# Second mixture of experts in tiles that serve two experts: 144 tiles in place of 160

## What is computed

```python
x = x + L0_gnn(layernorm(x), adj)
x = x + L0_ffn(layernorm(x))      # 8 experts, the two best of each row
x = x + L1_gnn(layernorm(x), adj)
x = x + L1_ffn(layernorm(x))      # 32 experts, the best of each row

def L1_ffn(x):
    idx = argmax(x @ router_w.T + router_b, axis=-1)
    h = relu(einsum('nd,ndh->nh', x, W1[idx]) + b1[idx])      # 128 -> 32
    return relu(einsum('nh,nhd->nd', h, W2[idx]) + b2[idx])   # 32 -> 128
```

## Time and profile before

| | us |
|---|---|
| median of 3 executions (1197.79 to 1203.39) | 1198.93 |
| the profiled execution, its time | 1197.08 |
| its span, first to last instruction | 1195.3 |
| TensorE busy in the span | 948.1 (79%) |
| VectorE busy | 791.0 (66%) |
| ScalarE busy | 708.2 (59%) |
| GpSimd busy | 781.6 (65%) |
| mean granted clock of TensorE, share of full speed | 0.837 |

### The profile page before, as it was taken

The page is one execution under the profiler, slowest core; times in us unless marked ns, Lnnn a source line. Parts: engine busy times, 40 slices in busy tenths (PEclk is TensorE's granted clock), DMA queues, the critical chain, the costliest instruction groups (busy, mean ns, idle before and its releaser), DMA issues. The chain is left out here.

```text
span 1195.3 us, 27365 instructions
## 1 busy us (share of the span) xinstructions
PE 948.1 (79%) x6789; PEld 839.2 (70%) x6789; DVE 791.0 (66%) x3492; ACT 708.2 (59%) x2414; POOL 781.6 (65%) x989
## 2 busy tenths in 40 slices
PE   5888988887179999999994899999960667666873
PEld 4677877776079999999994688888850555544653
DVE  6688898889459999999994378888873121121221
ACT  3998898886035656555552899999930333322431
POOL 4357777777617787877776048778785366666666
PEclk9999897987579999999997999999975655666555
DMA  9133432211367777777772113232213442223210
GB/s 207 37 120 118 139 102 61 60 51 38 95 180 207 203 205 206 208 203 207 196 203 60 36 51 87 76 86 76 60 42 109 109 111 83 74 82 85 64 35 8
DMA packets 147913, 130.88 MB, mean 109 GB/s; under 512 B 26450, under 2 KB 119484, under 8 KB 147760
## 3 DMA queue, kind: packets, MB, share of 16 engines
q1 hardware_dynamic: 125456, 93.02, 30.4%
q0 software_dynamic: 18272, 34.21, 8.4%
q10 hardware_dynamic: 4032, 1.89, 0.5%
HBM read 83.28 MB, written 49.61 MB: 111 GB/s over the span
## 5 line engine op out<-in xcount | busy, mean ns | idle before, releaser
L477 POOL DMA_INDIRECT xs<-staged,dst x256 | 258.9, 1011 | 77.6 <-issue 68.5
L1067 ACT ACTIVATE hT<-bank,wt 128x128 f32<-128x128 f32 x620 | 177.2, 369 | 133.4 <-PE bank L1274 81.4
L528 POOL DMA_INDIRECT out<-oq,xq x160 | 159.9, 999 | 112.2 <-DVE oq L978 66.3
L506 POOL DMA_INDIRECT x2d<-ob,xi x155 | 163.6, 1055 | 43.3 <-issue 29.1
L1260 PE MATMUL bank<-xnT,wt 128*128 128x128 f32 x1240 | 166.9, 278 | 0.7 <-issue 0.4
L1274 PE MATMUL bank<-w2s,hT 128*128 x1240 | 165.5, 276 | 0.7 <-DVE ob L951 0.5
L978 DVE SCALAR_TENSOR_TENSOR oq<-bank,xq 128x512 f32<-128x512 f32 x40 | 27.7, 692 | 197.1 <-remote 103.2
L1260 PEld LDWEIGHTS bank<-xnT,wt 128*128 128x128 f32 x1240 | 152.6, 194 | 3.1 <-issue 2.5
L1274 PEld LDWEIGHTS bank<-w2s,hT 128*128 128x128 f32 x1240 | 150.9, 192 | 1.8 <-issue 1.2
L1101 ACT ACTIVATE xnqT<-bank 128x512 f32<-128x512 f32 x40 | 23.9, 596 | 164.0 <-remote 71.0
L1016 ACT ACTIVATE p<-bank,nm 128x128 f32<-128x128 f32 x256 | 103.1, 403 | 19.1 <-DVE nm L699 13.9
(11 more groups left out here) (202 smaller groups left out, 2313.9 us busy)
## 6 DMA issues: line engine op xcount, KB each, us to landing
wt<-wpd SPq DMA_DIRECT2D x155, 258.0 KB
xq<-xs SPq DMA_DIRECT2D x160, 66.0 KB
xi<-xs SPq DMA_DIRECT2D x155, 66.0 KB
xb<-x2d SPq DMA_DIRECT2D x32, 258.0 KB
xb<-in_x SPq DMA_DIRECT2D x32, 256.0 KB
wpd<-w1c SPq DMA_DIRECT2D x56, 129.0 KB
xs<-staged,dst POOLq DMA_INDIRECT x256
out<-oq,xq POOLq DMA_INDIRECT x160
```

The costliest lines, as they stand in the source:

```text
L477: pool.indirect_dma_start(out=xs[l], out_offset=bass.IndirectOffsetOnAxis(ap=dst[b % ND][:, c:c + 1], axis=0), in_=stag[s][:, q, 0:ROW], i ...
L506: pool.indirect_dma_start(out=x2d, out_offset=bass.IndirectOffsetOnAxis(ap=xi[t % NXI][:, ID:ID + 1].bitcast(U32), axis=0), in_=ob[:, t % ...
L528: pool.indirect_dma_start(out=orow, out_offset=bass.IndirectOffsetOnAxis(ap=xq[j % NXQ][:, q, ID:ID + 1].bitcast(U32), axis=0), in_=oq[j % ...
L1067: last = act.activation(hT[t % 2][:, j, :], HID[t % 2][:, j, :], ACT.Gelu, bias=wt[t % NW][:, c:c + 1])
```

## The change

Two experts form a unit: the bucket of the even one grows down and that of the odd one grows up from the same point, so that they meet without a gap, and only the unit as a whole has a partly filled tile. 16 units give (16384 - 16) / 128 + 16 = 143 tiles, rounded up to 144, or 36 quads; there are 16 fills. A tile may hold rows of both experts. So each tile is worked out for both: the first matmuls have 97 output rows (32 of the one expert, 1 for the bias row, then 64 onward for the other), the second matmuls are done for rows 0 to 32 and for rows 64 to 96 of `hqT` into banks of their own, and VectorE multiplies each by the row's flag (`WLO` is 1 - odd, `WHI` is odd) and adds them. The flags are computed in `route1` and put into `staged` in `places`. The weights are packed by unit, W1, b1 and W2, b2 side by side, and ScalarE copies all 226 columns of a unit into `vq`, from which TensorE takes both operands' weights.

```diff
-NTILE = (NTOK // P + NB[0] - 1, NTOK // P + NB[1])
+NU = (NB[0], E1 // 2)
+NTILE = ((NTOK - NU[0]) // P + NU[0], ((NTOK - NU[1]) // P + NU[1] + 3) // 4 * 4)
+NFILL = (NB[0], E1 // 2)
+SPFILL = (16, 9)
-VW = H1 + 1 + P
+HW = 64 + H1 + 1
+VW = HW + 1 + P
-        vt = sb("vt", [P, E1, VW])
+        vt = sb("vt", [P, E1 // 2, VW])
-        NXQ, NOQ, NVQ = 12, 8, 5
+        NXQ, NOQ, NVQ = 10, 5, 4
-        TQ, HQ, YQ = bank[0], bank[1:3], bank[3:5]
+        TQ, HQ, YQ = bank[0], bank[1:3], (bank[3:5], bank[5:7])
...
-                for s in range(2):
-                    dve.memset(hqT[s][H1:H1 + 1, :], 1.0)
+                dve.wait_ge(sem("vt_zero"), 1)
+                dve.memset(vt[H1:H1 + 1, :, HW], 1.0)
+                dve.memset(vt[64 + H1:HW, :, HW], 1.0).then_inc(sem("vt_one"), 1)
...
                 dve.tensor_tensor(ge3(oh, k, E), rows(rev, k, E), wide(k1, k, E), ALU.is_equal).then_inc(sem("oh"), 1)
+                link(dve.tensor_copy(oddi[:, 0:k * G], k1[:, 0:k * G]))
+                link(dve.tensor_scalar(oddi[:, 0:k * G], oddi[:, 0:k * G], 1, None, ALU.bitwise_and))
+                mark(dve.tensor_copy(odd[:, 0:k * G], oddi[:, 0:k * G]))
...
+                    settled()
...
+                        dve.tensor_scalar(staged[:, s:s + run, :, WLO], t, -1.0, 1.0, ALU.mult, ALU.add)
+                        dve.tensor_copy(staged[:, s:s + run, :, WHI], t)
...
                     after(dve, "yq", j)
+                    for q in range(G):
+                        dve.tensor_scalar(ta_q[:, q, :], ya_q[:, q, :], row[:, q, WLO:WLO + 1], None, ALU.mult).then_inc(sem("ta_q"), 1)
+                    for q in range(G):
+                        after(dve, "ta_q", G * j + q)
+                        op = dve.scalar_tensor_tensor(tb_q[:, q, :], yb_q[:, q, :], row[:, q, WHI:WHI + 1], ta_q[:, q, :],
+                                                      ALU.mult, ALU.add)
+                    op.then_inc(sem("tb_q"), 1)
...
-                    dve.scalar_tensor_tensor(oq[j % NOQ][:, :, :], YQ[j % 2][:, :].rearrange("p (g f) -> p g f", g=G), 0.0, xq[j % NXQ][:, :, 0:P], ALU.max,
+                    after(dve, "tb_q", j)
+                    dve.scalar_tensor_tensor(oq[j % NOQ][:, :, :], tb_q[:, :, :], 0.0, row[:, :, 0:P], ALU.max,
                                              ALU.add).then_inc(sem("oq"), 1)
...
-                after(act, "hq_ps", j - NVQ)
-                after(act, "hqT", j - NVQ)
+                after(act, "yq", j - NVQ)
-                    last = act.activation(vq[j % NVQ][:, q, :], vflat[:, bass.ds(expert[4 * (j % 2) + q], H1 + 1)], ACT.Copy)
+                    last = act.activation(vq[j % NVQ][:, q, :], vflat[:, bass.ds(expert[4 * (j % 2) + q], VW)], ACT.Copy)
...
-                    if j % 2 == 0:
-                        expert = column(mybir.EngineType.PE, 1, 1, 4 * j, (E1 - 1) * VW)
-                    for q in range(4):
-                        last = pe.matmul(YQ[j % 2][:, q * P:(q + 1) * P], hqT[j % 2][0:H1 + 1, q * P:(q + 1) * P],
-                                         vflat[0:H1 + 1, bass.ds(expert[4 * (j % 2) + q] + (H1 + 1), P)], start=(q == 0), stop=(q == 3),
-                                         skip_group_check=True)
+                    for h in range(2):
+                        rows_ = slice(64 * h, 64 * h + H1 + 1)
+                        for q in range(4):
+                            last = pe.matmul(YQ[h][j % 2][:, q * P:(q + 1) * P], hqT[j % 2][rows_, q * P:(q + 1) * P],
+                                             vq[j % NVQ][rows_, q, HW + 1:VW], start=(q == 0), stop=(q == 3),
+                                             skip_group_check=True)
...
-                        last = pe.matmul(HQ[j % 2][0:H1, q * P:(q + 1) * P], vq[j % NVQ][:, q, 0:H1],
+                        last = pe.matmul(HQ[j % 2][0:HW, q * P:(q + 1) * P], vq[j % NVQ][:, q, 0:HW],
```

More of the change, by code:

```diff
@@ L226, in program @@
         filli = [sb(f"filli{l}", [P, E1], I32) for l in range(2)]
+        cntu = sb("cntu", [P, NU[1]])
         tabf = [sb(f"tabf{l}", [P, 4, 2]) for l in range(2)]
         tab = [sb(f"tab{l}", [8, P], I32) for l in range(2)]
-        hqT = [sb(f"hqT{s}", [H1 + 1, T]) for s in range(2)]
+        hqT = [sb(f"hqT{s}", [HW, T]) for s in range(2)]
         with ExitStack() as early:
@@ L272, in program @@
         xnqT = sb("xnqT", [P, T])
[L274 removed]
+        vq = [sb(f"vq{s}", [P, G, VW]) for s in range(NVQ)]
+        ta_q = sb("ta_q", [P, G, P])
+        tb_q = sb("tb_q", [P, G, P])
         oq = [sb(f"oq{s}", [P, G, P]) for s in range(NOQ)]
[L276 removed]
+        TQ, HQ, YQ = bank[0], bank[1:3], (bank[3:5], bank[5:7])
         def numbers(engine, ap, top):
@@ L311, in load, with fills @@
                 sp.dma_start(xb[n % NX][:, :, 0:(P, XW)[l]], xg[l][g]).then_inc(sem(f"x_in{n % NX}"), 16)
-            def fills(l, half):
+            def fills(l):
                 sp.wait_ge(sem("fill_row"), l + 1)
-                for r in numbers(mybir.EngineType.SP, filli[l][0:1, 16 * half:min(16 * half + 16, NB[l])], DUMMY[l] - P):
+                for r in numbers(mybir.EngineType.SP, filli[l][0:1, 0:SPFILL[l]], DUMMY[l] - P):
                     sp.dma_start(xs[l][bass.ds(r, P), :], pad[:, :]).then_inc(sem(f"filled{l}"), 16)
@@ L363, in _ @@
                                      w1c[:, pairs[k][h], :]).then_inc(sem("wpd"), 16)
-            fills(0, 0)
+            fills(0)
             scattered(0)
@@ L384, in _ @@
                 load(n)
-            fills(1, 0)
+            fills(1)
             scattered(1)
@@ L640, in numbers_ready @@
                 link(dve.tensor_copy(regf[:, :], regi[:, :]))
-                for l in range(2):
-                    dve.tensor_copy(first[l][:, :, 0], regf[:, 0:NB[l] // 2])
-                    dve.tensor_scalar(first[l][:, :, 1], regf[:, 0:NB[l] // 2], -1.0, -(REGION - 1.0), ALU.mult, ALU.add)
+                dve.tensor_copy(first[0][:, :, 0], regf[:, 0:NB[0] // 2])
+                dve.tensor_scalar(first[0][:, :, 1], regf[:, 0:NB[0] // 2], -1.0, -(REGION - 1.0), ALU.mult, ALU.add)
+                dve.tensor_scalar(first[1][:, :, 0], regf[:, :], -1.0, -(NTOK - 1.0), ALU.mult, ALU.add)
+                dve.tensor_scalar(first[1][:, :, 1], regf[:, :], float(NTOK), None, ALU.add)
                 dve.memset(sgn[:, :, 0], 1.0)
@@ L794, in tile_table @@
                 sh = shift[:, :, :].rearrange("p a b -> p (a b)")[:, 0:B]
[L795 to L798, removed]
+                U = NU[l]
+                if l == 0:
+                    link(dve.tensor_tensor(fillf[:, 0:B], end, s, ALU.mult))
+                    dve.tensor_tensor(filli[l][:, 0:B], fillf[:, 0:B], sh, ALU.add).then_inc(sem("fill_row"), 1)
+                    link(dve.tensor_tensor(cnt[:, 0:B], end, f, ALU.subtract))
+                    link(dve.tensor_scalar(cnti[:, 0:B], cnt[:, 0:B], P - 1.0, None, ALU.add))
+                else:
+                    ends = end.rearrange("p (k b) -> p k b", b=2)
+                    dve.tensor_copy(filli[l][:, 0:U], ends[:, :, 1]).then_inc(sem("fill_row"), 1)
+                    link(dve.tensor_tensor(cnt[:, 0:B], end, f, ALU.subtract))
+                    counts = cnt[:, 0:B].rearrange("p (k b) -> p k b", b=2)
+                    link(dve.tensor_tensor(cntu[:, 0:U], counts[:, :, 0], counts[:, :, 1], ALU.add))
+                    link(dve.tensor_scalar(cnti[:, 0:U], cntu[:, 0:U], P - 1.0, None, ALU.add))
+                B = U
                 for c in range(2):
```

64 lines of the change are left out of this document (43 added, 21 removed).

## The result

The changed kernel takes 1229.4 us (median of 4 runs, 1224.97 to 1230.72) beside 1199.35 us of the kernel before: 1.023 times as long, 95% interval 1.021 to 1.025. It is slower, as forecast, but by 30 us where 72 had been forecast. The profiled execution took 1228.77 us, its span is 1227.0.

The account below looks back on a forecast made before the run. The last stage was taken to be bound by a TensorE-VectorE loop in which no step overlaps another, 6.22 us per quad, not by GpSimd. 983 + 32 times the new 9.0 us loop gave 1271 us, range 1200 to 1325.

Parts of the forecast that it names:

- 9.0 us per quad: Last stage: the new loop of 8.44 us at the lower clock, + 1.0 for late completions, - 0.4 for the clock.
- 0.25 each, + 2.00 in the loop: Last stage, TensorE: eight further second-matmul passes per quad at 0.25 us each add 2.00 us to the loop.
- the halves overlap in the array: Rival: second matmuls stay near 2.1 us, loop 6.4 + 0.8 us, 1213 us in all; chance 0.06.
- late completions "+ 1.0": Last stage: matmul consumers starting late cost 1.32 us per quad before; less a quarter, 1.0 us is carried over.
- "- 0.4" for the clock: Last stage: with 16% of the time at the higher clock level, a quad gets 0.4 us shorter.
- The chain: Last stage, VectorE: four multiplications and four multiply-adds out of PSUM before `oq` add 1.94 us to the loop.
- Graph layer + 8.5: Second graph layer: added small routing operations cost 0.53 us, times 16, + 8.5 us; bounds 3 and 13.
- The head's - 1.3: Start of the kernel: the memset of `vt` has fewer columns, 4.38 to 3.07 us, saving 1.3 us.
- Seam - 5.5: Between graph layer and last stage: 16 fills for 32 end near 914, first load 5.5 us earlier; bounds - 4 and - 8.
- First rounds + 4: Start of the last stage: first `oq` comes 12.0 us after the first `xnq`, 8.0 before, so + 4.
- Copies, buffers and wider first matmuls at 0: Last stage: ScalarE's wider copies, fewer buffers and 97-column first matmuls lie off the loop and cost 0.
- TensorE stays at the higher clock: Rival, last stage: the loop is 5.77 us and the time 1168 us, faster than before; chance 0.10.

Follow-up runs that it names:

- e11: Changed kernel with the second matmuls ordered tile, then row half, so the halves alternate; 1202.6 us, 1.002 of a before of 1200.6.
- e8: Changed kernel without the second matmuls of rows 64 to 96, the second expert's product left out; 1180.9 us, 1.038 of a before of 1138.7.
- e10: Changed kernel with `xnq` ahead of the chain, second matmuls' row halves alternating and four flag operations for five; 1192.1 us, 0.993 of a before of 1200.6.
- e7: Kernel before plus eight VectorE operations of 128 columns per quad between second matmuls and `oq`; 1180.7 us, 1.036 of a before of 1138.7.
- the first set: The first runs of both kernels, with stalls: changed kernel 1229.4 us beside 1199.35 us of the kernel before.
- e6: The changed kernel, unchanged, run again in a set without stalls; 1214.3 us, 1.066 of a before of 1138.7.
- e5: The kernel before, unchanged, run again for its profile in a set without stalls; 1138.5 us.
- e9: Changed kernel with three more 16-bit matmuls of 512 columns per quad in TensorE's idle time; 1205.3 us, 1.006 of a before of 1200.6.
- e2: Changed kernel with TensorE's register loads back and the second matmuls of rows 0 to 32 reading W2 at a register's address; 1211.8 us, 1.065 of before.
- e3: Changed kernel with the next quad's `xnq` issued on VectorE ahead of the flags' chain; 1132.9 us, 0.997 of a before of 1137.1.
- e16: The edit of e7 repeated, one execution, on the chip number of e9 to e11; 1180.2 us beside a before of 1138.6.
- e17: Kernel before with `xnq` issued ahead of `oq`, one execution on the chip number of e9 to e11; 1137.9 us beside a before of 1138.6.

## Why the prediction was half right

*Direction and mechanism: right.* The loop, its order and what waits for what are as forecast; four rounds fewer don't pay for longer ones. TensorE stays at the lower clock (0.51) with idle time in each round. What was off is the size: three terms of the 9.0 us per quad were mis-sized, and the change cost 30 us for 72.

*The step that failed most: the second matmuls at "0.25 each, + 2.00 in the loop".* They took 3.13 us to the chain and not 4.12, so 0.99 us per quad, 32 us over 32 rounds. The prediction had a single boundary between the row halves pay off, where the trace has eight of the sixteen passes side by side (four of either half, started in pairs). The rival "the halves overlap in the array", at 0.06, was half true as the code stands and wholly true in e11. The Trainium skill (TensorE: Matmul & The Clock Gate, Part 3) says that weight loads overlap running matmuls of other rows; e8 and e11 agree (the eight further passes cost 1.03 us as the code stands and nothing when the halves alternate), and the reading that this touches only one boundary was the prediction's own.

*The second failed step: late completions "+ 1.0" carried over, and "- 0.4" for the clock.* Neither came, a net 0.6 us per quad or 19 us. An amount that couldn't be explained was treated as a property of the code, and the runs show it to be one of some sets, which strikes the kernel before and e10 but not the changed kernel's steady loop. This is also why the difference is 30 us there and 75.6 us elsewhere. That the forecast of + 72 comes near the second number is luck: its loop was 1.2 us too long, and its base was a before of 1197. The - 0.4 was carried over from the granted clock of 0.58 in the kernel before; in the changed kernel the clock is 0.51, so hardly a round has the higher level.

*The chain was sized too short*: 2.27 us for 1.94, + 0.33 per quad, 11 us. A multiplication by a factor per row starts 0.26 us after the one before (1110.14 to 1111.18 for four); the 0.20 was read from a copy. In e7, where the factors are constants, the chain adds 1.78.

These three make 9.0 into 7.74, against 7.80 measured; the remaining 0.06 is in the rounding of the steps.

*The smaller terms.* Graph layer + 8.5: right in the first set, + 8.6 from the first to the last scatter of the second graph layer (209.3 to 217.9 us), though + 11.8 in e6 beside e5. The head's - 1.3 was there at the start (first scatter 75.2 and 73.0) and was gone when the second graph layer began (its first scatter 706.8 and 707.6). Seam - 5.5: - 4.9, but not as told: the fills did not end near 914, SP issued the last at 929.1, in a stall. The rate of 0.61 us per fill behind that term was itself read in a stall: SP's fills stand 1.27 us apart there (903.7 to 922.7) and 0.52 in e6. Without stalls the seam shrinks by only 2.2 us (9.0 to 6.8) and the last scatter sets it. First rounds + 4: + 3.2; first interval 10.32 for 12.6, last two 4.97 and 2.87 for 6.0 and 4.1, since all of these hold second matmuls. Copies, buffers and wider first matmuls at 0: right, ScalarE's copies (0.38 us each) start with the chain and nobody waits.

*The clock.* The rival "TensorE stays at the higher clock" did not come: 0.51. e9 shows that there is a lever toward it: 1.4 us of extra matmuls in the idle time (0.8 at the higher clock) win back more than they take.

## What to carry to other kernels

Before a loop's unexplained surplus goes into a forecast, look at instructions that should always last the same, such as register instructions ahead of DMAs: if their maximum is twenty times their median, the surplus may belong to the moment of the run and not to the code, and it need not pass over to the changed kernel. Run the kernel before again at another time too: here one chip number gave 1200.6 and 1138.6 us. In a serial loop look first at which engine's program order closes it: one loop bound moved (`xnq` ahead of the chain) was worth 79 us (e2 to e3), more than the 75 us that the change costs without stalls. And if two row halves of the array are used, issue them alternately.

## What the runs showed of the hardware that was not expected

- Sixteen passes with 33-row weights take 3.13 us to their reader when eight of one row half come first, and 2.13 us when the halves alternate: the time of eight.
- Three idle-time matmuls of 512 columns per quad raise the granted clock of the last stage from 0.51 to 0.68, and the kernel takes 1205.3 us for 1229.4 (sets with stalls, not the same set).
- In some sets of runs engines stall together: register instructions of 29 to 37 ns last 0.70 us and more, matmuls start up to 10.7 us late with nothing that the profile shows to wait for (e10), and the kernel before takes 1200 us and not 1138. GpSimd's issue goes on meanwhile. It isn't fixed to a chip: chip 3 had 1200.6 us with e9 to e11 and 1138.6 with e16 and e17.
- Multiplications of 128 columns out of PSUM by a factor per row follow each other after 0.26 us (the changed kernel, four in 1.04 us), those by a constant after 0.20 (e7, four in 0.80 us).
